# Routing a first MoE layer in groups of 1, 2, 2, 2, 1 batches, the last group inside the layer's first shared units

## The reference

```python
x = x + mamba(_layernorm(x), ...)             # selective scan, gated, out projection
x = x + moe0(_layernorm(x), ...)              # 14 routed experts, top 2, and 2 shared ones
x = x + attention(_layernorm(x), ...)         # causal
x = x + moe1(_layernorm(x), ...)              # 8 routed experts, top 2, and 1 shared one

# moe0, for N = 4096 tokens
gates = softmax(xf @ router_w)
top_v, top_i = top_k(gates, 2)
masked = zeros.at[n, top_i].set(top_v); masked /= masked.sum(-1) + EPS
def _ffn(xn, rw, W1, W2):                     # 128 -> 256 -> 128
    return silu((xn * rsqrt(mean(xn * xn) + RMS_EPS) * rw) @ W1) @ W2
out = sum over e of masked[:, e] * _ffn(xf, rms_w[e], w1[e], w2[e]) + sum of the 2 shared ones
```

## Time and profile before

| | |
|---|---|
| median of 3 runs | 1148.78 us |
| profiled execution | 1151.23 us, span 1149.5 us |
| granted TensorE clock, mean | 0.884 of 2.4 GHz |
| routing stage | about 506 to 611 us |
| MoE stage of layer 0 | about 611 to 784 us |
| busy in the span | TensorE 900.5 us (78%), VectorE 843.4, ScalarE 758.9, POOL 711.5 |

### The profile page before, as it was taken

The page is one execution under the profiler, slowest core; times in us unless marked ns, Lnnn a source line. Parts: engine busy times, 40 slices in busy tenths (PEclk is TensorE's granted clock), DMA queues, the critical chain, the costliest instruction groups (busy, mean ns, idle before and its releaser), DMA issues.

```text
span 1149.5 us, 16137 instructions
## 1 busy us (share of the span) xinstructions
PE 900.5 (78%) x4818; PEld 684.7 (60%) x4818; DVE 843.4 (73%) x1510; ACT 758.9 (66%) x1507; POOL 711.5 (62%) x536
## 2 busy tenths in 40 slices
PE   1999487787787787877666999995778857999980
PEld 0764266666565565666565777773455646777760
DVE  6424589899999999945747777764677657888866
ACT  2347688888888788833424888884656635787870
POOL 1130299898998999960777544427764564477750
PEclk9996599999999999868967999996887857999995
DMA  4000586765777567700112577612110114455316
GB/s 113 5 10 5 136 199 211 218 176 173 247 192 186 193 209 209 175 19 1 47 54 86 131 202 204 184 61 66 52 37 32 38 45 123 139 170 159 111 45 182
DMA packets 127880, 139.21 MB, mean 121 GB/s; under 512 B 16054, under 2 KB 86181, under 8 KB 127796
## 3 DMA queue, kind: packets, MB, share of 16 engines
q1 hardware_dynamic: 117892, 121.15, 37.8%
q0 software_dynamic: 9088, 16.94, 4.6%
q10 hardware_dynamic: 816, 0.11, 0.1%
HBM read 76.86 MB, written 63.11 MB: 122 GB/s over the span
## 4 chain that ended last, share of the span: by engine, by line
PE 54%; DVE 16%; ACT 14%; POOL 7%; issue 6%; DMA 2%; DVEq 0%; SPq 0%; ACTq 0%; POOLq 0%; PEldq 0%
PE ps L1617 10%; PE ps L1618 9%; PE ps L1619 9%; DVE arena L1253 7%; POOL arena L615 5%; PE ps L1705 3%; PE ps L1675 3%; PE ps L1890 3%; ACT arena L828 2%; PE ps L1849 2%; ACT arena L818 2%; PE ps L1713 2%; DVE x L1516 2%; PE ps L1664 2%; ACT arena L817 2%
## 5 line engine op out<-in xcount | busy, mean ns | idle before, releaser
L615 POOL TENSOR_TENSOR arena<-arena 128x1024 f32<-128x1024 f32 x128 | 298.9, 2361 | 34.5 <-DVE arena L1253 30.8
L1253 DVE TENSOR_TENSOR_SCAN arena<-arena,ps 128x1024 f32<-128x1024 f32 x128 | 284.9, 2270 | 21.8 <-PE ps L1705 13.9
L640 POOL DMA_INDIRECT xs<-hx,slot x128 | 127.6, 997 | 100.7 <-DVE slot L1331 64.0
L1675 PE MATMUL ps<-ident,arena 128*128 128x128 f32 x1088 | 148.4, 287 | 20.4 <-POOL arena L615 17.5
L1675 PEld LDWEIGHTS ps<-ident,arena 128*128 128x128 f32 x1088 | 130.7, 148 | 27.8 <-POOL arena L615 23.8
L828 ACT ACTIVATE arena<-arena,bT 128x256 f32<-128x256 f32 x344 | 145.4, 494 | 0.0
L1705 PE MATMUL ps<-ident,arena 128*128 128x128 f32 x688 | 101.6, 295 | 53.7 <-DVE arena L1253 39.4
L1705 PEld LDWEIGHTS ps<-ident,arena 128*128 128x128 f32 x688 | 80.8, 150 | 96.2 <-ACT arena L828 79.1
L663 POOL DMA_INDIRECT yd<-yb,dest x92 | 94.6, 1028 | 53.6 <-ACT yb L935 31.3
L817 ACT ACTIVATE arena<-softplus_dt,Aneg 128x512 f32<-128x512 f32 x128 | 91.7, 716 | 40.1 <-DVE arena L1253 40.1
L1465 DVE TENSOR_TENSOR h_lo<-hs,h_hi 128x512 fp32r<-128x512 f32 x90 | 70.9, 801 | 43.9 <-ACT h_hi L914 43.6
(11 more groups left out here) (283 smaller groups left out, 2146.0 us busy)
## 6 DMA issues: line engine op xcount, KB each, us to landing
xs<-zero SPq DMA_DIRECT2D x16, 2340.0 KB, 11.6
arena<-bc_rows SPq DMA_DIRECT2D x64, 512.0 KB, 5.3
x_blk<-xs SPq DMA_DIRECT2D x52, 260.0 KB, 2.8
w_raw<-in_L_ffn_w SPq DMA_DIRECT2D x58, 128.0 KB
ys<-yb SPq DMA_DIRECT2D x29, 256.0 KB, 2.6
big<-yd SPq DMA_DIRECT2D x8, 512.0 KB, 3.5
w_raw<-in_L_ffn_Wg SPq DMA_DIRECT2D x23, 128.0 KB
w_raw<-in_L_ffn_Wu SPq DMA_DIRECT2D x23, 128.0 KB
```

Source lines behind the costliest of these rows:

```text
L615: nc.gpsimd.tensor_tensor(hc[M % 3], h[N % 3], row.unsqueeze(1).to_broadcast([P, NG, L]), ALU.mult)\
L640: pool.indirect_dma_start(out=xs, out_offset=bass.IndirectOffsetOnAxis(ap=slot[:, q, t:t + 1], axis=0), in_=hx[:, t, :], in_offset=None).t ...
L1253: nc.vector.tensor_tensor_scan(h[N % 3].rearrange("p g t -> p (g t)"), dA[N % 2].rearrange("p g t -> p (g t)"), ps[N % 2][:, :, :].rearran ...
L1675: return nc.tensor.matmul(out_, in_, ident[:, :], is_transpose=True, start=first_, stop=False, skip_group_check=True)
```

## The change

- Layer 0 is routed in five groups: batch 0; 1 and 2; 3 and 4; 5 and 6; 7. The loops have five iterations, one for each group; routing of group G-1 lies in iteration G as before. The `project_z` and `silu_z` of later batches follow the new groups.
- The routing of the last group (batch 7) lies in the unit loop of the MoE: on ScalarE `scale_rows` after unit 2's silu and `take_routed` after unit 3's; on TensorE `columns_of` after `down(2)`, `logits_of` after `down(3)`, `count_group` after `down(4)`, `count_all` after `down(5)`; on VectorE `pick_group` ahead of `low_h(4)`, `place_group` ahead of `low_h(5)`, `take_counts` and `lay_out` ahead of `low_h(6)`. It has its own PSUM banks, in `ps[2]`.
- `low_x(0)` is issued in the last iteration, behind `pick_group` of batches 5 and 6 and ahead of `add_o(7)`.
- Barrier 7 is gone. Six shared batches are ahead of the blocks and two behind.
- In layer 1 a group is one batch, as before; helpers are only rewritten.

```diff
-        SPAN = (2, 1)
-        GTS = [n * TPB for n in SPAN]
-        NGRS = [NB // n for n in SPAN]
+        GROUPS = [[[0], [1, 2], [3, 4], [5, 6], [7]], [[b] for b in range(NB)]]
+        NGRS = [len(g) for g in GROUPS]
...
-        BARRIERS = (1, 3, 4, 7, 8, 11, 12)
+        BARRIERS = (1, 3, 4, 8, 11, 12)
...
-        SHARED_FIRST = (4, 4)
+        SHARED_FIRST = (6, 4)
...
+        def tiles_of(k, G):
+
+            return slice(GROUPS[k][G][0] * TPB, (GROUPS[k][G][-1] + 1) * TPB)
+
+        def group_of(b):
+
+            return [G for G in range(NGRS[0]) if b in GROUPS[0][G]][0]
+
+        def batches(G):
+
+            return GROUPS[0][G] if 0 <= G < NGRS[0] else []
+
+        LAST = NGRS[0] - 1
+
+        def routed_bank(b):
+
+            return ps[2][:, 0, :] if b == NB - 1 else TRN[b % 2]
+
+        def rank_bank(k, G):
+
+            return ps[2][:, 1, :] if k == 0 and G >= LAST else RKS[k]
+
+        def gates_until(G):
+
+            return max(2, batches(min(G + 1, NGRS[0] - 1))[-1] + 1)
+
+        def gates_ahead(G):
+
+            return range(gates_until(G - 1), gates_until(G)) if G < NGRS[0] else ()
...
@@ ScalarE and TensorE, the loops of the routing stage @@
-            for G in range(NGRS[0] + 1):
-                now = range(2 * G, 2 * G + 2) if G < NGRS[0] else ()
-                past = range(2 * G - 2, 2 * G) if G else ()
-                after = range(2 * G + 2, 2 * G + 4) if G + 1 < NGRS[0] else ()
+            for G in range(NGRS[0]):
+                now, past, after = batches(G), batches(G - 1), gates_ahead(G)
...
@@ ScalarE, moe @@
                 for U in range(units(k) + 3):
                     if U < units(k):
                         (silu_gate if k else silu_twice)(U)
+                    if k == 0 and U == 2:
+                        for b in batches(LAST):
+                            scale_rows(b)
+                    if k == 0 and U == 3:
+                        for b in batches(LAST):
+                            take_routed(b)
...
-            barrier(act, 7)
             moe(0)
...
@@ VectorE, the loop of the routing stage @@
+            def low_of_first_batch():
+
+                dve.wait_ge(mo[0]["xh"], 1)
+                nc.vector.tensor_tensor(x_lo[:, 0, :], xT[:, 0, PAD:], x_hi[:, 0, :], ALU.subtract)\
+                    .then_inc(mo[0]["xl"], 1)
+
+            for G in range(NGRS[0]):
+                now = batches(G)
                 for b in now:
                     gate_y(b)
                 if G:
                     pick_group(0, G - 1)
+                if G == LAST:
+                    low_of_first_batch()
                 for b in now[0:1]:
                     add_o(b)
                 if G:
                     place_group(0, G - 1)
                 for b in now[1:2]:
                     add_o(b)
+                if now:
                     scales(G)
...
-            take_counts(0)
...
@@ VectorE, moe @@
-                low_x(0)
-                lay_out(k)
+                if k:
+                    low_x(0)
+                    lay_out(k)
                 for U in range(units(k) + AHEAD[k] + 2):
+                    if k == 0 and U == 4:
+                        pick_group(0, LAST)
+                    if k == 0 and U == 5:
+                        place_group(0, LAST)
+                    if k == 0 and U == 6:
+                        take_counts(0)
+                        lay_out(0)
                     if U < units(k):
...
-            barrier(dve, 7)
...
@@ TensorE, behind the loop of the routing stage and in moe @@
-            count_all(0)
-
...
                     if U < units(k):
                         down(U)
+                    if k == 0 and U == 2:
+                        for b in batches(LAST):
+                            columns_of(b)
+                    if k == 0 and U == 3:
+                        for b in batches(LAST):
+                            logits_of(b)
+                    if k == 0 and U == 4:
+                        count_group(0, LAST)
+                    if k == 0 and U == 5:
+                        count_all(0)
                     j = job_until(k, U - 1)
...
-            barrier(pe, 7)
             pe.wait_ge(shared_split, 1)
```

More of the change, by code:

```diff
@@ L633, in send @@
             def send(k):
-                GT = GTS[k]
                 for G in range(NGRS[k]):
-                    pool.wait_ge(ln[1 + 2 * k]["norm"], SPAN[k] * (G + 1))
+                    w = tiles_of(k, G)
+                    pool.wait_ge(ln[1 + 2 * k]["norm"], GROUPS[k][G][-1] + 1)
                     pool.wait_ge(gt[k]["slot"], G + 1)
-                    for t in range(G * GT, (G + 1) * GT):
+                    for t in range(w.start, w.stop):
                         for q in range(2):
@@ L1041, in _ @@
                         scaled_rows(3, t - 1)
-                        if group_with_end(1, t - 1) is not None:
-                            router_root(group_with_end(1, t - 1))
+                        router_root(t - 1)
                     if i == 1 and valid(t + 2):
@@ L1283, in add_o @@
                 batch_stats(b, link)
-            def tiles_of(k, G):
-                return slice(G * GTS[k], (G + 1) * GTS[k])
             def pick_group(k, G):
-                E, GT, w = EXPERTS[k], GTS[k], tiles_of(k, G)
+                E, w = EXPERTS[k], tiles_of(k, G)
+                GT = w.stop - w.start
                 s = gt[k]
@@ L1317, in pick_group @@
                 by_row(M1, F3, best2, ALU.is_equal)
-                hot = onehot[:, G * GT * E:(G + 1) * GT * E].rearrange("p (t e) -> p t e", e=E)
+                hot = onehot[:, w.start * E:w.stop * E].rearrange("p (t e) -> p t e", e=E)
                 nc.vector.tensor_tensor(hot, M0, M1, ALU.add).then_inc(s["hot"], 1)
             def place_group(k, G):
-                E, GT, w = EXPERTS[k], GTS[k], tiles_of(k, G)
+                E, w = EXPERTS[k], tiles_of(k, G)
+                GT = w.stop - w.start
                 s = gt[k]
                 dve.wait_ge(s["prefix"], G + 1)
-                place = RKS[k][:, 256:256 + GT * E].rearrange("p (t e) -> p t e", e=E)
+                place = rank_bank(k, G)[:, 256:256 + GT * E].rearrange("p (t e) -> p t e", e=E)
                 chosen = gl0[:, SCRATCH, w, 0:E]
@@ L1568, in _ @@
                     shifts(3, t - 1)
-                    if group_with_end(1, t - 1) is not None:
-                        router_square(group_with_end(1, t - 1))
+                    router_square(t - 1)
                 if G is not None:
@@ L1776, in columns_of @@
                 for q in range(TPB):
-                    last = nc.tensor.transpose(TRN[b % 2][:, q * P:(q + 1) * P], hrow[:, b * TPB + q, :], ident[:, :])
+                    last = nc.tensor.transpose(routed_bank(b)[:, q * P:(q + 1) * P], hrow[:, b * TPB + q, :], ident[:, :])
                 last.then_inc(ln[1]["tr"], 1)
@@ L1782, in logits_of @@
                 pe.wait_ge(rms_ready, 1)
-                at_least(pe, gt[0]["slot"], b // 2)
+                at_least(pe, gt[0]["slot"], group_of(b))
                 for q in range(TPB):
-                    at_ = (b % 2 * TPB + q) * E0
-                    last = nc.tensor.matmul(RKS[0][:, at_:at_ + E0], xT[:, b, PAD + q * P:PAD + (q + 1) * P], wr[:, :],
+                    at_ = ((b - batches(group_of(b))[0]) * TPB + q) * E0
+                    last = nc.tensor.matmul(rank_bank(0, group_of(b))[:, at_:at_ + E0], xT[:, b, PAD + q * P:PAD + (q + 1) * P], wr[:, :],
                                             start=True, stop=True)
@@ L1790, in count_group @@
             def count_group(k, G):
-                E, GT = EXPERTS[k], GTS[k]
+                E, w = EXPERTS[k], tiles_of(k, G)
+                GT = w.stop - w.start
                 pe.wait_ge(gt[k]["hot"], G + 1)
-                hot = onehot[:, G * GT * E:(G + 1) * GT * E]
-                at_ = RKS[k][:, 256:256 + GT * E]
+                hot = onehot[:, w.start * E:w.stop * E]
+                at_ = rank_bank(k, G)[:, 256:256 + GT * E]
                 whole = at_.rearrange("p (t e) -> p t e", e=E)
@@ L1808, in count_all @@
                 pe.wait_ge(gt[k]["cum"], NGRS[k])
-                nc.tensor.matmul(RKS[k][:, 480:480 + E], ones[:, :], cum[:, 0:E], start=True, stop=True)\
+                nc.tensor.matmul(rank_bank(k, NGRS[k])[:, 480:480 + E], ones[:, :], cum[:, 0:E], start=True, stop=True)\
                     .then_inc(gt[k]["prefix"], 1)
```

26 lines of the change are left out of this document (11 added, 15 removed).

## The result

The changed kernel takes 1163.48 us (median; 1157.73 to 1168.55) beside 1148.44 us (1146.61 to 1149.73) for the kernel before on the same chip: ratio 1.011, interval 1.0084 to 1.0137. It is 1.1% slower. The forecast was 1162.0, in a range of 1149 to 1171, and "slower" had 0.80.

What follows compares the result with a forecast made beforehand. Routing was taken as bound by a chain, not an engine, and the MoE proper by TensorE. The terms -9.6 + 17.7 + 5.1 gave +13.2 us, so 1162.0, in a range of 1149 to 1171.

Steps and rivals of the forecast that it cites:

- A: Routing up to the first shared matmul: the MoE starts 9.6 us earlier, bounds -19.4 and -6.3.
- Item 1: In A, the first group's `scales` starts when batch 0 is added, not batch 1: -4.1 us.
- item 2: In A, the second routing iteration scales one batch instead of two: -3.1 us.
- Item 3: In A, from the last statistics to the first shared matmul: 14.0 us at half clock instead of 16.4, so -2.4.
- full clock in routing: Rival, chance 0.12: routing iterations keep full clock, the start moves by -19.4 us, total 1150.2.
- B: Batch 7's routing inside the shared units, up to `down(6)`: +15.7 us, with half clock afterwards +17.7.
- third rival: Chance 0.15: half clock in every piece between the stalls and 5 us behind them, B +25, total 1169.3.
- C: Six shared batches ahead: layer 0's output fetch starts 12.6 us later against the MoE's end, costing +5.1, bounds 0 and 6.5.
- Hidden with 14 us to spare: In C, the first block's rows land at 644 us and TensorE asks for them at 658.

Runs made afterwards that it cites:

- second profile: The changed kernel run and profiled once more, nothing edited: 1161.54 us, ratio 1.0098 to the kernel before.
- e4: Against the kernel before: groups of 1, 2, 2, 2, 1 batches, all routed ahead of the MoE, barrier 7 and four shared batches first kept: 1158.16 us, ratio 1.0067.
- e2: The kernel before with only six shared batches ahead of the blocks: 1156.40 us, ratio 1.0042.
- e1: The changed kernel with four shared batches ahead of the blocks again: 1156.53 us, ratio 1.0056.
- e9: The changed kernel with four shared batches first and `lay_out` spread, only one unit's low parts ahead of `table`: 1159.56 us, ratio 1.0087.
- e3: The changed kernel with `lay_out` cut into pieces and the units' low parts between them: 1161.33 us, ratio 1.0112.
- e10: As e9, with SP issuing the rows of blocks 0, 1 and 2 ahead of the weights of blocks 1, 2 and 3: 1154.37 us, ratio 1.0026.
- e8: e3 run once more, beside the changed kernel: 1163.07 us, ratio 1.0104.
- e11_four_first_again: e1 run once more, the changed kernel with four shared batches first: 1157.99 us, ratio 1.0074.

## Why the forecast was right

The sum of the differences is +13.7 between the spans: -13.0 up to the first shared matmul, +32.6 to the first block, -5.9 to the last combine, 0.0 behind it. The forecast's terms, each beside its measure:

- **A, -9.6: was -13.0** (-13.6 in the second profile), inside the bounds -19.4 and -6.3. Item 1 had -4.1 and was -4.4 (525.22 against 529.58). The next interval, item 2, is 17.3 against 23.2: -5.9 where -3.1 was forecast, at a clock of 0.93 between 530 and 550 us (0.74 before). The two behind it, forecast as unchanged, are 22.65 and 20.42 against 19.2 and 22.5, +1.3 together. Item 3 is 12.28 at a clock of 0.76 against 16.4: -4.1, where 14.0 at half clock gave -2.4. This is the term that was mis-sized, on the side that helps; the rival "full clock in routing" needed -14 and nearly got it. How much it is differs from one execution to the next: nine profiles with this routing have the first shared matmul between 593.3 and 600.5, three with the old one between 610.9 and 612.8. What the gain rests on is the last routing's removal; groups of another size by themselves give nothing (e4).
- **B, +17.7: was +20.0.** From the first `up` to `down(6)` 36.84 against 18.75, +18.1 where +15.7 was forecast. Item by item: to `down(0)` 7.91 (8.1); to `pick_group` 9.22 (8.0); to `down(4)` 3.72 (4.0); to `up(8)` 4.6 (4.3); to the counts 3.0 (1.9); to `down(6)` 8.36 (8.2). The two misses are the two pieces in which TensorE works between stalls; the matmul at 605.76 takes 0.79 and those behind it 0.63 up to 611.5, against 0.39 at full clock, so there were 6 us of half clock where 4 were assumed (and 6.3 at full clock with 4 us of half clock makes 8.3, not the 8.0 of the sum). Behind the last stall half clock cost +2.0, as forecast. The rule of the Trainium skill ("TensorE: Matmul & The Clock Gate", section on HAM oscillation) that stood behind the third rival is borne out in part: behind each of the four waits (3.33, 2.96, 1.86 and 6.92 us) the matmuls have the half-clock duration of 0.63, but the stretch's mean granted clock is 0.64, neither all half nor the 0.78 of before.
- **C, +5.1: was +6.7 by the columns** (12.6 in front, 5.9 back; +4.5 with the second profile, 8.1 back), and +4.8 and +4.5 by the ratios of e2 and e1. Its own figures, 806.3 against 801.38, made the first delay 4.9 and not the 4.5 that entered the sum. The mechanism is the one forecast: the second combine waits 5.14 us (5 to 7 forecast), the third 0.29 (0.6), and with four batches ahead both are gone.
- **"Hidden with 14 us to spare"** for the rows of the first block. It holds in the changed kernel: no matmul waits for `x_blk`. But the step named the time (rows at 644) without the chain that makes it. SP's four weight loads are in series behind `table`, and two of the six shared batches are what covers them once VectorE's stalls are shorter (e9: 4.1 us of wait with four). This is where the experiments needed a second theory.
- The waits on `h_lo` were forecast as three or four, 15 us or more in total; they are three, 13.2 us in total, and only with one more of 1.9 us on `x_lo` is it 15.1.

The terms lean in opposite directions, A by -3.4, B by +2.3 and C by +1.6. So part of the closeness of 1162.0 to 1163.5 is luck; the signs and the order of the terms are not.

What stays open: how much of VectorE's full stretch in the spread kernels comes from the longer operations beside POOL's splitting, which no run isolated. And whether e4's slower routing at a clock of 0.7 belongs to its order or to the chance of that execution.

## What to carry to other kernels

A stage moved from ahead of a dense phase into it is hidden only if the dense phase's own feeders have room: here each step of the routing on VectorE stood in front of a `h_lo`, so both engines took turns waiting, and TensorE's 15 us of stall with the half clock behind it (B, 20.0 us) were paid for 13 gained (beside the same groups with all routing ahead, e4, 19 for 18). Spreading such steps does not help where the feeder is busy throughout: e3's VectorE was, for 20.3 of 21 us. Before a stall is removed, look for what else becomes ready at that time, a queue like SP's in particular, whose order was harmless as long as the stall was there: reordering its loads was worth 5.2 us (e9 against e10), spreading the work behind the stall nothing (e3, e8). And here more work in front of the blocks left less behind them to cover the fetch: two shared batches moved ahead cost 4.5 to 4.8 us.

## What the hardware showed that was not expected

- Executions of one kernel spread by 4.5 to 13 us (the groups alone from 1153.67 to 1162.99, e11_four_first_again from 1154.47 to 1167.58, the kernel before from 1144.64 to 1153.99). In the profiles the same two-batch iteration takes 19.2 us at a granted clock of 1.00 and 23.49 at 0.71 (the groups alone). Differences of 2 or 3 us between single profiles can't be read off the span. Between two profiles of one kernel the distance from the first shared matmul to the first block agrees better (49.2 and 49.3; 59.8 and 59.9; 62.6 and 61.9), and from there to the MoE's last unit it is the same to 0.1 us (128.06 and 128.06; 140.52 and 140.52). From there to the last combine it is not: 108.6 and 106.4 us in the changed kernel's two.
- Some VectorE operations take 1.4 to 6 times as long beside POOL's splitting of the weights (in e3_layout_spread 0.97 to 1.09 for 0.69, 1.74 for 0.68, 1.30 for 0.22). It is not all of them: `x<-x,ps` takes its usual 0.67 us at 642.58, beside a cast of POOL's. Beside POOL's indirect transfers `h_lo` takes 0.68 (at 617.87 in the changed kernel).
